# Graph kernel, building the adjacency: bases behind the first key gathers, root one-hots from ScalarE in octs 3 to 22, four statistics in oct 4

## The reference

```
deg_out = segment_sum(ones, src)          deg_in = segment_sum(ones, dst)
msg = x[src]                              agg = segment_sum(msg, dst, 3125)
mean, var of each row of x                (layer norm)
```

## Time and profile before

| | us |
|---|---|
| median of three executions | 775.46 |
| profiled execution | 770.75 |
| its span (first to last instruction) | 769.0 |
| TensorE busy in the span | 700.8 (91%) |
| VectorE busy | 563.5 (73%) |
| ScalarE busy | 424.6 (55%) |
| GpSimd busy | 32.7 (4%) |

### The profile page before, as it was taken

The page is one execution under the profiler, slowest core; times in us unless marked ns, Lnnn a source line. Parts: engine busy times, 40 slices in busy tenths (PEclk is TensorE's granted clock), DMA queues, the critical chain, the costliest instruction groups (busy, mean ns, idle before and its releaser), DMA issues. The chain is left out here.

```text
span 769.0 us, 19001 instructions
## 1 busy us (share of the span) xinstructions
PE 700.8 (91%) x7912; PEld 658.5 (86%) x7912; DVE 563.5 (73%) x1273; ACT 424.6 (55%) x730; POOL 32.7 (4%) x36
## 2 busy tenths in 40 slices
PE   6699988899989999999998499999856999997997
PEld 6586665699979999999998389999746999996997
DVE  7999999944555555334445899999798999987642
ACT  7768887700041232122235698999378899955500
POOL 6032220000000000000000000000000000000000
PEclk9669999999989999999999799999967999999999
DMA  6000000069900000000004107665270399989710
GB/s 161 6 16 12 7 6 1 7 233 414 416 26 2 1 2 2 2 1 2 14 27 133 37 20 235 223 216 194 65 240 18 70 209 209 213 168 230 158 39 26
DMA packets 121241, 78.07 MB, mean 102 GB/s; under 512 B 97840, under 2 KB 115942, under 8 KB 121023
## 3 DMA queue, kind: packets, MB, share of 16 engines
q1 hardware_dynamic: 120612, 75.45, 34.7%
q0 software_dynamic: 384, 0.94, 0.4%
q10 hardware_dynamic: 154, 0.40, 0.1%
HBM read 30.51 MB, written 25.78 MB: 73 GB/s over the span
## 5 line engine op out<-in xcount | busy, mean ns | idle before, releaser
L2110 PE MATMUL banks<-loose,adjacency 128*128 128x194 f16 x1250 | 212.5, 247 | 0.0
L882 PE MATMUL banks<-y_sb,adjacency 128*128 128x192 f16 (+1 forms) x1875 | 165.3, 248 | 1.0 <-DVE h_sb L1129 0.8
L882 PEld LDWEIGHTS banks<-y_sb,adjacency 128*128 128x128 f16 x1875 | 160.8, 99 | 1.8 <-DVE h_sb L1129 1.0
L2109 PE MATMUL banks<-x_sb,gat_masks 128*128 128x194 f16 x820 | 141.6, 249 | 1.8 <-DVE adjacency L2024 1.7
L2080 ACT ACTIVATE gat_masks<-y_sb,node_scalars 128x640 bf16<-128x640 f32 x164 | 122.0, 829 | 3.9 <-PEq L141 3.9
L2110 PEld LDWEIGHTS banks<-loose,adjacency 128*128 128x128 f16 x1250 | 122.7, 98 | 0.4
L814 ACT ACTIVATE adjacency<-counts 128x850 f16<-128x850 f32 x92 | 80.3, 884 | 27.6 <-PE counts L663 26.5
L2109 PEld LDWEIGHTS banks<-x_sb,gat_masks 128*128 128x128 f16 x820 | 80.5, 98 | 2.7 <-DVE y_sb L2020 2.1
L1360 ACT ACTIVATE y_sb<-banks 96x256 f32<-96x256 f32 x50 | 19.1, 382 | 93.6 <-PE banks L1392 93.6
L2020 DVE TENSOR_TENSOR gat_masks<-gat_masks,adjacency 128x1920 f16<-128x1920 bf16 (+1 forms) x64 | 64.3, 1008 | 6.6 <-ACT gat_masks L2080 6.4
L2024 DVE TENSOR_TENSOR adjacency<-adjacency,gat_masks 128x1920 f16<-128x1920 f16 (+1 forms) x64 | 64.0, 1008 | 0.4
(11 more groups left out here) (290 smaller groups left out, 1122.7 us busy)
## 6 DMA issues: line engine op xcount, KB each, us to landing
kept_adj<-adjacency SPq DMA_DIRECT2D x5, 4000.0 KB, 32.1
adjacency<-kept_adj SPq DMA_DIRECT2D x25, 800.0 KB, 5.6
y_sb<-a_dst_rows SPq DMA_DIRECT2D x10, 320.0 KB, 3.7
residual<-h_sb SPq DMA_DIRECT2D x5, 240.0 KB, 2.0
kept_x<-x_sb SPq DMA_DIRECT2D x1, 1200.0 KB, 5.1
loose<-residual SPq DMA_DIRECT2D x5, 240.0 KB, 3.5
x_sb<-kept_x SPq DMA_DIRECT2D x5, 240.0 KB, 4.9
x_sb<-in_x SPq DMA_DIRECT2D x4, 240.0 KB
```

The source lines that it names most:

```text
L882: return nc.tensor.matmul(k.ps[:, j % G, 0:cols], k.ADJ[:, i, j * P:(j + 1) * P], y[:, i, 0:cols], start=i == 0, stop=i == NT - 1)
L2109: nc.tensor.matmul(bank[:, 0:2 * BC], over_of(x)[:, q * P:(q + 1) * P], features[0][:, i, :], start=i == 0, stop=False)
L2110: return nc.tensor.matmul(bank[:, 2 * BC:4 * BC], under_of(x)[:, q * P:(q + 1) * P], features[1][:, i, :], start=False, stop=i == NT - 1)
```

## The change

Three things change, in `build_adjacency` alone.

1. GpSimd issues the gathers of loads 0 and 1 first and writes the bases behind the second. There are eight of them now instead of six. On ScalarE the table load for Abs_reciprocal_sqrt and the wait for the bases move from ahead of store 0 to behind store 3, where `past(1)` is added. A gather from load 3 on waits for the `past` two loads back.
2. FROM_OCT goes from 6 to 3, and the last oct is no longer left out. TensorE has bands for octs 3, 4, 5 and 22 more, ScalarE `alone` for the same, VectorE the last set of octs 3, 4, 5 without unit 4, and eight short sets instead of ten in the last oct.
3. The statistics of tiles 21 to 24 move from the run ahead of the first unpacking to oct 4, between the first and the second set of codes.

```
--- before.py
+++ after.py
@@ -55,7 +55,7 @@
 ALONE = WT - 1
 BAND_AFTER = 1
 STEEPEST = 2.0 ** 60
-FROM_OCT = FIRST[2] // OCT
+FROM_OCT = LOADS[0] // OCT
 ONES_ROW = UNITS
 LATER = 2
 BEGINS_AT, BEGINS_IN, SPLIT_AFTER, SPREAD_AT, STARTS_AFTER, TURN_AT = 2, 4, 3, 10, 4, 17
@@ -70,7 +70,7 @@
 SHIFTS = 4
 TILE_WINDOWS = SHIFTS * MOST
 MAIN_STEPS, EARLY_STEPS = 13, 7
-MEASURED = (2, 4)
+MEASURED = (2, 4, 21)
 LEADING = MAIN_STEPS
 PLACES = LEADING + WT * 2 * TILE_WINDOWS
 
@@ -342,22 +342,23 @@
         for u in range(WT):
             pool.tensor_scalar(by_unit[:, :, u, :], by_unit[:, :, u, :], float(FROM[u]), None,
                                ALU.add).then_inc(own_ready, 1)
-        pool.wait_ge(base_ready, 1)
-        for load in range(EARLY_LOADS, len(LOADS)):
-            pool.tensor_scalar(load_bases[0:UNITS, load:load + 1], own_base[0:UNITS, :], float(CODES * FIRST[load]), -1.0,
-                               ALU.add, ALU.mult).then_inc(bases_ready, 1)
         pool.wait_ge(first_keys_out, 16)
         for load in range(len(LOADS)):
             if load >= 2:
                 pool.wait_ge(keys_turned, load - 1)
-                if load - 2 >= EARLY_LOADS:
-                    pool.wait_ge(beyond_ready, load - 1 - EARLY_LOADS)
+                if load > 2:
+                    pool.wait_ge(beyond_ready, load - 2)
                 pool.wait_ge(keys_out, key_writes)
             pool.wait_ge(starts_ready, min(load, EARLY_LOADS) + 1)
             rows = WT * LOADS[load]
             pool.indirect_dma_start(window_keys[0:rows, load % 2, :], None,
                                     d.keys[0:FIRST_KEYS * EF, :] if load < EARLY_LOADS else d.keys[:, :],
                                     bass.IndirectOffsetOnAxis(ap=starts[0:rows, load:load + 1], axis=0)).then_inc(window_in[load % 2], 16)
+            if load == EARLY_LOADS - 1:
+                pool.wait_ge(base_ready, 1)
+                for other in range(len(LOADS)):
+                    pool.tensor_scalar(load_bases[0:UNITS, other:other + 1], own_base[0:UNITS, :], float(CODES * FIRST[other]), -1.0,
+                                       ALU.add, ALU.mult).then_inc(bases_ready, 1)
 
     @block.vector
     def _(dve):
@@ -464,7 +465,7 @@
         dve.wait_ge(own_ready, WT)
         chain(dve.tensor_tensor(own_diagonal, own[0:UNITS, :], k.ident[0:UNITS, 0:UNITS], ALU.mult))
         dve.tensor_reduce(own_base[0:UNITS, :], own_diagonal, axis=AX, op=ALU.add).then_inc(base_ready, 1)
-        statistics(MEASURED[1], NT)
+        statistics(MEASURED[1], MEASURED[2])
 
         def unpack(load):
 
@@ -513,13 +514,15 @@
                     starts_of(slice(EARLY_LOADS, len(LOADS)), starts_ps, EARLY_LOADS + 1)
                 if o < octs - 1:
                     for n, some in enumerate(SETS):
+                        if n == 1 and o == STARTS_AFTER:
+                            statistics(MEASURED[2], NT)
                         codes(load, o, some[0], len([u for u in some if not (u == ALONE and o >= FROM_OCT)]), 0, OCT)
                         if n == 0 and load > 0 and load + 1 < len(LOADS) and o == octs_of(load)[-1]:
                             unpack(load + 1)
                             dve.wait_ge(keys_unpacked, load + 2)
                 else:
                     for half in range(2):
-                        for u in range(WT):
+                        for u in range(ALONE):
                             codes(load, o, u, 1, half * QUAD, QUAD)
                 if o == 0:
                     dve.wait_ge(keys_out, key_writes)
@@ -652,12 +655,12 @@
             o, first = p // (OCT // 2), 2 * p % OCT
             pe.wait_ge(rows_hot, o + 1)
             for u in range(WT):
-                if u == ALONE and FROM_OCT <= o < octs - 1:
+                if u == ALONE and FROM_OCT <= o:
                     pe.wait_ge(alone_hot, o - FROM_OCT + 1)
                 elif o < octs - 1:
                     pe.wait_ge(codes_hot, len(SETS) * o + [u in some for some in SETS].index(True) + 1)
                 else:
-                    pe.wait_ge(codes_hot, len(SETS) * o + first // QUAD * WT + u + 1)
+                    pe.wait_ge(codes_hot, len(SETS) * o + first // QUAD * ALONE + u + 1)
                 for i in range(2):
                     at = AT[u] + (first + i) * EVEN_WIDE[u]
                     last = nc.tensor.matmul(counts[:, 2 * (p % HELD) + i, FROM[u]:FROM[u] + WIDE[u]],
@@ -668,7 +671,7 @@
         def band(o):
 
             load = max(n for n in range(len(LOADS)) if FIRST[n] <= o * OCT)
-            pe.wait_ge(beyond_ready, load - EARLY_LOADS + 1)
+            pe.wait_ge(beyond_ready, load)
             if o == FROM_OCT:
                 pe.wait_ge(bands_in, 16)
                 pe.wait_ge(bands_ready, MOST // OCT)
@@ -695,7 +698,7 @@
         lags, degrees_done = range(MAIN_STEPS + WT), 0
         for p in range(PAIRS):
             pair(p)
-            if p % (OCT // 2) == BAND_AFTER and FROM_OCT <= p // (OCT // 2) + 1 < octs - 1:
+            if p % (OCT // 2) == BAND_AFTER and FROM_OCT <= p // (OCT // 2) + 1 < octs:
                 band(p // (OCT // 2) + 1)
             if p >= DEGREES_FROM:
                 for _ in range(2 - p % 2):
@@ -789,14 +792,13 @@
             at = (q * WT + ALONE) * OCT
             nc.scalar.activation(bands[0:UNITS, q, :, :], k.ident_h[0:UNITS, at:at + OCT].unsqueeze(2)
                                  .to_broadcast([UNITS, OCT, WIDE[ALONE]]), ACT.Copy).then_inc(bands_ready, 1)
-        act.preload_act_table(ACT.Abs_reciprocal_sqrt)
-        act.wait_ge(bases_ready, len(LOADS) - EARLY_LOADS)
 
         def past(load):
 
             act.wait_ge(window_in[load % 2], 16 * (load // 2 + 1))
-            if load >= EARLY_LOADS + 2:
+            if load >= 2:
                 act.wait_ge(beyond_banded, FIRST[load - 1] // OCT - FROM_OCT)
+                act.wait_ge(keys_turned, load - 1)
             rows = LOADS[load] * WT
             nc.scalar.activation(beyond[load % 2][0:rows, :],
                                  window_keys[0:rows, load % 2, :].rearrange("p (n e) -> p n e", e=2)[:, :, 1],
@@ -813,7 +815,11 @@
             act.wait_ge(counted, p + 1)
             nc.scalar.activation(k.ADJ[:, :, 2 * p * W:2 * (p + 1) * W].rearrange("p t (b o) -> p t b o", o=W),
                                  counts_of(2 * (p % HELD), 2), ACT.Copy, scale=UNIT).then_inc(stored, 1)
-            if p % (OCT // 2) == BAND_AFTER and FROM_OCT <= p // (OCT // 2) + 1 < octs - 1:
+            if p == OCT // 2 - 1:
+                act.preload_act_table(ACT.Abs_reciprocal_sqrt)
+                act.wait_ge(bases_ready, len(LOADS))
+                past(1)
+            if p % (OCT // 2) == BAND_AFTER and FROM_OCT <= p // (OCT // 2) + 1 < octs:
                 alone(p // (OCT // 2) + 1)
             for load in range(EARLY_LOADS, len(LOADS)):
                 if p == turned_at(load - 1) + 1:
```

21 lines of the change are left out of this document (11 added, 10 removed).

## The result

The changed kernel took 768.39 us in the median of 13 executions (766.72 to 770.02), the kernel before 772.18 us in 13 beside them (769.44 to 778.33): a ratio of 0.9944, with a 95% interval from 0.9918 to 0.997. Forecast were 775.2 us (0.2 faster) and a range from 769.0 to 778.8.

The account below looks back on a forecast made before the run. VectorE was taken as the bound from 53.7 to 141.2 us, carrying earlier gains unchanged. 2.25 − 1.0 − 1.3 + 0.41 − 0.13 = 0.2 us faster, put on the median 775.46: about 775.2 us, range 769.0 to 778.8.

Parts of the forecast that it names:

- first unpacking: VectorE's first unpacking of keys, after the earlier gather and the filler matmuls: 17.4 instead of 19.68 us, gain 2.25 us.
- scan in oct 3: VectorE's scan behind the last begin matmuls, which band(3) precedes in TensorE's queue: gains 1.6 us instead of 2.25.
- rows of oct 5: VectorE's start of oct 5, held by TensorE's pair 15: at 48.55 instead of 49.81 us, 1.26 earlier.
- unpacking of load 2: VectorE's unpacking in the middle of oct 5, waiting for ScalarE's cast: at 53.85 us, a gain of −0.07 us.
- rows of oct 6: VectorE's start of oct 6, after oct 5's short set adds 0.41 us: 0.34 us earlier, carried through the long stretch.
- the moment of the clock's rise: TensorE's granted clock rises from 0.50 to 1.00 at about 50.6 us, taken as the same in the changed kernel.
- −1.0: Octs 2 to 4: new band matmuls in TensorE's queue delay VectorE, giving back 1 us of the 2.25.
- −1.3: Oct 5: alone(5) ahead of ScalarE's cast makes VectorE wait for load 2's keys, giving back 1.3 us.
- rival of 0.20: TensorE's clock rises one stretch earlier, alone(5) is hidden: gain 1.6 us, 773.9 us; chance 0.20.
- that of 0.08: VectorE is never held up: gain 3.1 us, 772.4 us; chance 0.08.
- the last oct: End of the building: alone(22) puts 0.72 us among ScalarE's first four stores, 0.59 free, so the end is 0.13 later.
- that rival: A 1.38 us drain at ScalarE's moved table load delays VectorE's oct 3: 0.6 us slower, 776.1 us; chance 0.05.

Follow-up runs that it names:

- e12: The kernel before, unchanged, profiled once more in a single execution: 775.4 us.
- e7: The changed kernel with band(3) behind the last begin matmuls of pair 9 instead of ahead of them: median 768.4 us.
- e8: The changed kernel with the last oct's root one-hots given back to VectorE: median 769.2 us.
- e2: The changed kernel with its start as before (bases of loads 2 to 7 ahead of the gathers) and all statistics ahead: median 775.3 us.
- e3: The changed kernel with all 21 statistics ahead of the first unpacking: median 773.2 us.
- e5: The kernel before with only the statistics of tiles 21 to 24 moved into oct 4: median 771.6 us, ratio 0.9985.
- e11: The changed kernel once more, unchanged, for a second profile: median 768.4 us, ratio to before 0.9962.
- e4: The kernel before with two more matmuls of 400 columns behind pair 9, whose result nobody reads: median 775.4 us.
- e6: The changed kernel with the four statistics ahead of the first set of oct 4 instead of behind it: median 770.1 us.
- e1: The kernel before with only GpSimd's order changed, gathers of loads 0 and 1 first and the bases behind them: median 773.6 us, ratio 1.0008.

## Why the prediction was wrong

The sum was 0.2 us; the building gained 3.2 in the two profiles and the kernel 3.8 in the median. How much earlier VectorE was than before, at each point of the sum:

| point | forecast, us | measured, us |
|---|---|---|
| first unpacking | 2.25 | 2.72 |
| scan in oct 3 | 1.6 | 1.83 |
| rows of oct 5 | 1.26 | 2.52 |
| unpacking of load 2 | −0.07 | 2.64 |
| rows of oct 6 | 0.34 | 3.07 |
| end | 0.2 | 3.22 |

Two steps failed: the moment of the clock's rise, on which the two terms −1.0 and −1.3 hung, and a term for load 2's gather, which was not in the sum.

**The step with the clock.** "I take the same moment for the changed kernel": the rise at 50.6 us was read from one execution and taken as fixed. In the profiles the first rise behind 25 us comes at 29 to 49.5 us, falls back in some, and two profiles of one kernel (before and e12) differ. In both profiles of the changed kernel it was at 39.5, and VectorE waited neither for pair 15 nor for the cast: of the 1.0 us for TensorE 0.2 was given back (2.72 to 2.52), and the 1.3 for the cast was 0. Where the clock rose at 48.5 and 49.5 the waits were there (e7: 1.15, 0.36 and 0.36 us ahead of the starts, the rows of oct 5 and the cast; e8: 0.74, 0.36 and 0.32), so the mechanism was right for that case. What sets the moment stays open: neither the bands nor the early start has been shown to do it, and with one or two profiles of a kernel neither is ruled out. The prediction had this as its rival of 0.20 ("the clock rises one stretch earlier", gain 1.6) and, without any wait, that of 0.08 (3.1). That 3.1 lies so near the 3.2 is in part luck: the start brought 0.47 more and the last oct 0.27 more than in that sum, and the 0.89 lost up to the scan are not in it.

**The missing term: load 2's gather.** The sum had no term for how long this gather takes. The prediction cited a rule that points at one, said that no row separates it from other causes, and went on. The rows were there: 0.99 to 4.63 us of GpSimd time for eight like gathers, and this one of the kernel before, which began ahead of VectorE's wait of 0.42 us (49.39 to 49.81) and ended 0.4 us behind it:

```profile
47.53 2.71 POOL L358 DMA_INDIRECT window_keys<-edge_keys,starts  x1 [29.16 <-DVE starts L449]
```

The runs showed both sides: 6.2 to 6.6 us and a stall of about 4 in three profiles in which VectorE had no pause between the starts and the keys (e2, e3, e12), 1.1 us in all seven with four statistics between two sets (changed, e5, e7 to e11), 2.7 and 1.8 without a pause in e4 and e6. The change's third part, costed at +0.65 us or hidden, is the one that takes the upper group away: by the means, before loses 772.87 − 771.04 = 1.8 us to that group (771.04 is the mean of its nine lower times; 1.0 to 3.0 us in the three later sets), and the rest of the gain is 771.04 − 768.36 = 2.7 us. In the two profiles of the table the keys were waited for in neither, so none of their 3.2 us is the gather's.

The Trainium skill (SBUF — State Buffer, SBUF: two separate sides) says that GpSimd can't write the descriptors of a DMA that it issues while VectorE holds their common port with a two-port instruction, such as a copy in fp32, and that the port is an exclusive lock. That the held gathers end 0.80 to 0.88 us after one of VectorE's instructions agrees with such a lock. But the comparisons here are `tensor_tensor` in float16 with both inputs in SBUF, for which that section names the lock only against a GpSimd instruction that reads SBUF; that they hold up an indirect gather is measured here. Which port is held no run shows.

**The start.** Forecast 2.25, measured 2.72 us: mechanism as said, filler and turn adjoining. The filler's own time hangs on the clock too, 4.21 us here and 5.09 in e1 and e8, and the first unpacking falls at 16.96, 18.35 and 18.18 us: the gain is 1.3 to 2.7 us. The gather came at 12.92 instead of 12.4, which the filler hid.

**Scan, one-hots, table, end.** The wait ahead of the scan came (0.81 us; forecast 0.65). Oct 5 took 5.47 us instead of 6.02. The table load between stores follows store 3 (28.53 + 0.88 = 29.41) at 29.43 and has its next ACTIVATE directly behind it, at 30.73 after 29.43 + 1.28: no drain on either side, that rival is out. The last oct, forecast as a loss of 0.13 us, was a gain of 0.14: alone(22) took its 0.72 and the 0.59 of waiting was gone, but the eight stores took 1.69 + 5.34 = 7.03 us instead of 3.65 + 3.66 = 7.31. Why they were shorter is not shown.

**Base.** The sum was made against a lower-group execution and then put on a median of three runs of which two were in the upper group. Two times 5 to 8 us above the profile were a fact to be explained before forecasting; the prediction took them as spread. In the set of 13 the median of before was 772.18, so 3.3 of the 6.8 us between the forecast 775.2 and the measured 768.4 come from the base.

## To carry to other kernels

Ask of each gather that GpSimd issues what VectorE runs in the microsecond behind it: here a pause between comparisons in 16 bits always let it through, without one only sometimes, and a wait that looks like a loss may be what lets it pass. If the times of a tuned kernel fall in two groups, profile one of each before costing anything. And a clock level read from one execution is a case with a chance, not a constant.
